# An AdaLN block with a routed and a shared feed-forward layer on one core: five experts instead of four are scattered to tables of their own, and the tables are loaded whole

## What is computed

```python
h = _layernorm(x, axis=-1) * (1 + cb) + sb          # after a causal running mean was added to x
logits = xf @ gate_weight.T                          # 8 experts
scores = softmax(logits).T
vals, idx = top_k(scores.reshape(-1), 2 * S)         # the 8192 best (expert, token) pairs of all
h = gelu(xf @ W1[e] + b1[e]); y = h @ W2[e] + b2[e]  # for each chosen pair, weighted by its score
shared = gelu(xf @ Ws1 + bs1) @ Ws2 + bs2            # for every token
x = x + gb * (routed + shared)
```

## Time and profile before

| | us |
|---|---|
| median of 3 executions | 339.92 |
| lowest, highest | 336.08, 343.24 |
| the profiled execution | 338.42 |
| its span | 336.5 |

### The profile page before, as it was taken

How to read it: one execution, slowest core, us unless ns; L and a number is a source line. 1 busy time by engine, 2 the same in 40 slices (tenths; PEclk the granted TensorE clock), 3 DMA queues, 4 the chain that set the end, 5 groups by cost and what they waited for, 6 DMA issues and landing times.

```text
span 336.5 us, 4143 instructions
## 1 busy us (share of the span) xinstructions
PE 259.8 (77%) x1033; PEld 138.9 (41%) x1033; DVE 177.7 (53%) x774; ACT 139.8 (42%) x238; POOL 196.5 (58%) x243
## 2 busy tenths in 40 slices
PE   4789777999999999999795996999999888700000
PEld 1657765443445454544352452544434334500000
DVE  2799865767656476567567567649351323100000
ACT  2768977454334434444333243344543443300000
POOL 7567862000026556567778770787878686868560
PEclk9999997999999999999999699799999999965555
DMA  7912991149962113123164272466884233333320
GB/s 190 341 37 78 314 317 76 31 99 228 133 254 59 36 41 105 44 51 114 52 211 137 78 265 83 162 230 181 301 294 39 25 33 31 32 39 32 31 24 8
DMA packets 25760, 40.72 MB, mean 121 GB/s; under 512 B 7544, under 2 KB 17599, under 8 KB 24704
## 3 DMA queue, kind: packets, MB, share of 16 engines
q1 hardware_dynamic: 17218, 31.09, 31.4%
q0 software_dynamic: 8384, 9.23, 15.2%
q10 hardware_dynamic: 126, 0.04, 0.0%
HBM read 22.62 MB, written 17.73 MB: 120 GB/s over the span
## 4 chain that ended last, share of the span: by engine, by line
PE 38%; POOL 24%; issue 11%; DMA 11%; DVE 9%; ACT 3%; POOLq 1%; SPq 0%; DVEq 0%; ACTq 0%
POOL out_dram L1166 14%; PE U L1311 8%; PE Y L1351 7%; POOL R L1141 6%; DMA INV<-sums_scratch 5%; PE U L1317 5%; PE Y L1355 5%; DMA out_dram<-YO,IDXB 4%; POOL sums_scratch L1154 3%; PE R1b L1199 2%; PE R L1199 2%; PE Y L1241 2%; DVE GJ L934 2%; PE R L1455 2%; DMA CST<-in_consts_dram 1%
## 5 line engine op out<-in xcount | busy, mean ns | idle before, releaser
L1141 POOL DMA_INDIRECT R<-rows_scratch,IDXB x68 | 69.0, 1014 | 70.8 <-DVE IDXB L950 52.2
L523 ACT ACTIVATE HF<-U,COL 128x512 f32<-128x512 f32 x96 | 65.8, 687 | 87.4 <-PE U L1317 56.0
L1166 POOL DMA_INDIRECT out_dram<-YO,IDXB x36 | 56.4, 1566 | 21.6 <-DMA out_dram<-YO,IDXB 12.1
L1317 PE MATMUL U<-XT,XW 128*128 128x512 f32 x128 | 66.6, 608 | 2.9 <-issue 2.9
L1355 PE MATMUL Y<-HF,XW 128*128 128x512 f32 x128 | 66.8, 614 | 0.0
L1154 POOL DMA_INDIRECT sums_scratch<-YO,IDXB x32 | 34.1, 1066 | 18.0 <-issue 9.1
L1311 PE MATMUL U<-H2F,WS 128*128 128x512 f32 x64 | 34.8, 627 | 0.0
L994 DVE SCALAR_TENSOR_TENSOR YO<-R1b,R,GBR 128x128 f32<-128x128 f32 x64 | 18.0, 344 | 30.6 <-DMA out_dram<-YO,IDXB 26.2
L1317 PEld LDWEIGHTS U<-XT,XW 128*128 128x128 f32 x128 | 23.1, 195 | 26.8 <-issue 23.6
L1351 PE MATMUL Y<-HF,WS 128*128 128x512 f32 x64 | 33.8, 610 | 0.0
L1355 PEld LDWEIGHTS Y<-HF,XW 128*128 128x128 f32 x128 | 23.2, 197 | 19.2 <-issue 19.2
(11 more groups left out here) (217 smaller groups left out, 369.1 us busy)
## 6 DMA issues: line engine op xcount, KB each, us to landing
sums_scratch<-R SPq DMA_DIRECT2D x8, 1024.0 KB, 6.4
INV<-sums_scratch SPq DMA_DIRECT2D x16, 512.0 KB, 4.9
XW<-in_wx_dram SPq DMA_DIRECT2D x10, 512.0 KB, 5.7
XW<-in_L_attn_x_dram SPq DMA_DIRECT2D x8, 256.0 KB, 6.9
rows_scratch<-HT SPq DMA_DIRECT2D x8, 256.0 KB, 4.0
out_dram<-X SPq DMA_DIRECT2D x4, 512.0 KB, 7.0
R<-rows_scratch,IDXB POOLq DMA_INDIRECT x68, 2.7
INV<-in_inv_dram SPq DMA_DIRECT2D x3, 256.0 KB, 6.7
```

The source lines that it names most:

```text
L523: eng.activation(HF[:, g % RING, :], UB[g % 2][:, :], ACT.Gelu_apprx_tanh, bias=B1[:, at:at + 1]).then_inc(M["a_gelu"], 1)
L1141: eng.indirect_dma_start(XG[:, v % XR, s, :], None, rows_dram, bass.IndirectOffsetOnAxis(ap=IDXB[:, v, s:s + 1], axis=0)).then_inc(M[f"ld_ ...
L1166: eng.indirect_dma_start(out, bass.IndirectOffsetOnAxis(ap=IDXB[:, v, s:s + 1], axis=0), YO[:, v % YR, s, :], None, compute_op=ALU.add).th ...
L1317: eng.matmul(bank[:, :], weights(v, 0, c, 0), XT[:, v % 2, :], start=True, stop=True).then_inc(M["pe_up"], 1)
```

## The change

A fifth expert gets a table (NTAB 5), so units 0 to 9 scatter plainly and units 10 to 16 accumulate. Two more clears of 1 MB are issued ahead. Each quarter of a table has a buffer of its own: two in INV, two in H2F, over shared blocks 0 to 3, whose last reader is waited for; so a whole table is loaded at once, a quarter waiting only for the add of the same quarter of the table before. The adds stand at the steps that ADD_AT names and the loads at LOAD_AT. The jobs are reordered: shared block 6 follows unit 9 and shared block 7 follows unit 10, so `close(6)` and `close(7)` come later, at steps 71 and 79. The last table's adds stand at steps 78 and 79. The lists come each five half steps. Six units are gathered ahead of the first scatter (AHEAD 6), then two or three DMAs for each scatter (5 for two), and behind the scatter of unit 9 all that are left, 22.

```diff
--- before.py
+++ after.py
@@ -36,12 +36,11 @@
 ROW = D + E + 1
 NPAD = BLK
 XR = 12
-NTAB = 4
+NTAB = 5
 YR = 4
-TBR = 2
 PAIR = 2 * BLK
 NP = NB // 2
-AHEAD = 9
+AHEAD = 6
 WR = 4
 LAG = 2
 
@@ -53,8 +52,8 @@
 H0 = max(BIT_AT) + 1
 
 ALONE = NMAIN - 4
-JOBS = ([(0, b) for b in range(NB - 2)] + [(1, 0), (1, 1), (0, NB - 2), (1, 2), (1, 3), (0, NB - 1)]
-        + [(1, v) for v in range(4, NU)])
+JOBS = ([(0, b) for b in range(NB - 2)] + [(1, v) for v in range(2 * NTAB)]
+        + [(0, NB - 2), (1, 2 * NTAB), (0, NB - 1)] + [(1, v) for v in range(2 * NTAB + 1, NU)])
 SJ = [JOBS.index((0, b)) for b in range(NB)]
 UJ = [JOBS.index((1, v)) for v in range(NU)]
 FIRST = NC * UJ[0]
@@ -66,18 +65,31 @@
 
 FAR = 32768.0
 K_MASK, K_TIE, K_CUM, K_DQ, K_IDX = 0, 1, 2, 5, 6
-MASK_AT = {K_IDX + 2 + 6 * (v - 1): v for v in range(1, NMAIN)}
+MASK_AT = {K_IDX + 2 + 5 * (v - 1): v for v in range(1, NMAIN)}
 EXTRA = 10
-K_OVER = K_IDX + 2 + 6 * (EXTRA - 1) + 3
+K_OVER = K_IDX + 2 + 5 * (EXTRA - 1) + 3
 OV_DONE = 10
 
 TR = 5
 CLOSE_AT = {21: 0, 23: 1, 25: 2, 27: 3, 28: 4, 29: 5, NC * SJ[6] + 7: 6, NC * SJ[7] + 7: 7}
 PART0 = 5
 
+
+ADD_AT = {}
+for e, at in enumerate((UJ[6], UJ[8], SJ[6], SJ[7])):
+    for q in range(NP):
+        ADD_AT[NC * (at + q // 3) + q % 3] = [(e, q)]
+ADD_AT[NC * UJ[11] + 2] = [(NTAB - 1, 0), (NTAB - 1, 1)]
+ADD_AT[NC * UJ[11] + 3] = [(NTAB - 1, 2), (NTAB - 1, 3)]
+
+LOAD_AT = {NC * UJ[5] + 3: 0, NC * UJ[7] + 3: 1, NC * UJ[9] + 3: 2, NC * UJ[10] + 3: 3, NC * UJ[11] + 1: 4}
+STORE_AT = NC * UJ[11] + 2
+
+ADDED = {6: 3 * NP, 7: 4 * NP}
+CLOSED = [6, 6, 6, 7, 8]
+
 XC0 = NB - 3
 NHT = 3
-PER_GAP = 2
 
 ROWS_AT = {3: NB - 3, 5: NB - 2, 7: NB - 1}
 
@@ -86,13 +98,13 @@
 
     if v >= 2 * NTAB - 1:
         return NT * NMAIN
-    return max(NT * AHEAD + PER_GAP * (v + 1), NT * (v + 4))
+    return NT * AHEAD + 5 * (v + 1) // 2
 
 
 
 SEMS = """ld_cst ld_uc ld_few ld_rows ld_x0 ld_x1 ld_x2 ld_x3 ld_x4 ld_x5 ld_x6 ld_x7 ld_wmod ld_ws ld_irow ld_inv1 ld_inv
 ld_wu0 ld_wu1 ld_wu2 ld_wu3 ld_xg0 ld_xg1 ld_xg2 ld_xg3 ld_xg4 ld_xg5 ld_xg6 ld_xg7 ld_xg8 ld_xg9
-ld_tb0 ld_tb1 ld_xg10 ld_xg11
+ld_tb0 ld_tb1 ld_tb2 ld_tb3 ld_xg10 ld_xg11
 st_z st_tz st_ht0 st_ht1 st_ht2 st_sc st_out st_sc0 st_sc1 st_sc2 st_sc3
 pe_inv pe_few pe_cols pe_mod pe_gbc pe_cbr pe_t1 pe_t3 pe_t4 pe_t6 pe_lg pe_up pe_dn pe_out pe_sum pe_tie pe_cum pe_dq
 pe_ov pe_idx pe_xt pe_yt pe_stc
@@ -166,7 +178,6 @@
         ZERO = sb("ZERO", [P, BLK])
 
         INV = sb("INV", [P, NT, BLK])
-        TB = INV[:, :, :].rearrange("p (k t) c -> p k (t c)", k=TBR)
         WS = sb("WS", [P, 2 * F])
         WMOD = sb("WMOD", [P, 6 * D])
         ROWS = sb("ROWS", [P, P])
@@ -193,6 +204,9 @@
         CLEAR = R1[:, 3 * PAIR:5 * PAIR]
         X2 = sb("X2", [P, NB, BLK])
         H2F = sb("H2F", [P, S])
+
+        TB = [INV[:, 2 * q:2 * q + 2, :].rearrange("p t c -> p (t c)") for q in range(2)] + [
+            H2F[:, q * PAIR:(q + 1) * PAIR] for q in range(2)]
         HT = sb("HT", [P, NHT, BLK])
         HF = sb("HF", [P, RING, BLK])
         TMP = sb("TMP", [P, TR, BLK])
@@ -360,12 +374,16 @@
                 if q == 0:
                     for v in (2 * e, 2 * e + 1):
                         eng.wait_ge(M[f"st_sc{v % YR}"], 64 * (v // YR + 1))
-                if NP * e + q >= TBR:
-                    eng.wait_ge(M["v_add"], NP * e + q - TBR + 1)
+                if e:
+                    eng.wait_ge(M["v_add"], NP * (e - 1) + q + 1)
+                elif q < 2:
+                    eng.wait_ge(M["v_ct"], NB)
                 else:
-                    eng.wait_ge(M["v_ct"], NB)
-                eng.dma_start(TB[:, q % TBR, :].rearrange("p (t c) -> p t c", c=D),
-                              by_partition(sums[e])[:, 2 * q * NT:2 * (q + 1) * NT, :]).then_inc(M[f"ld_tb{q % TBR}"], 16)
+                    eng.wait_ge(M["pe_up"], NC * SJ[3] + NC)
+                    eng.wait_ge(M["pe_t6"], NB)
+                    eng.wait_ge(M["pe_lg"], NB)
+                eng.dma_start(TB[q].rearrange("p (t c) -> p t c", c=D),
+                              by_partition(sums[e])[:, 2 * q * NT:2 * (q + 1) * NT, :]).then_inc(M[f"ld_tb{q}"], 16)
 
             def store_base(q):
                 eng.wait_ge(M["v_add"], NP * (NTAB - 1) + q + 1)
@@ -391,15 +409,12 @@
                     load_expert(v // 2 + WR - 1)
                 if c == 2 and v == NS - 4:
                     load_pair(NS)
-                if c == 3 and v >= 4 and v % 2 == 0 and v // 2 - 2 < NTAB:
-                    for b in range(TBR):
-                        load_sums(v // 2 - 2, b)
-                if c == 0 and v >= 5 and v % 2 and v // 2 - 2 < NTAB:
-                    for b in range(TBR, NP):
-                        load_sums(v // 2 - 2, b)
-                if c == 3 and v == 2 * NTAB + 3:
-                    for b in range(NP):
-                        store_base(b)
+                if s in LOAD_AT:
+                    for q in range(NP):
+                        load_sums(LOAD_AT[s], q)
+                if s == STORE_AT:
+                    for q in range(NP):
+                        store_base(q)
             eng.wait_ge(M["v_used"], 1)
             used = eng.value_load(USED[0:1, 0:1], min_val=NMAIN, max_val=NU)
             pair(NMAIN)
@@ -786,16 +801,19 @@
             def close(b):
                 eng.wait_ge(M["pe_out"], b + 1)
                 eng.wait_ge(M["v_x2"], b + 1)
+                if b in ADDED:
+                    eng.wait_ge(M["v_add"], ADDED[b])
                 eng.tensor_tensor(X2[:, b, :], RB[1][:, :], X2[:, b, :], ALU.add).then_inc(M["v_out"], 1)
 
             def add_sums(e, q):
-                eng.wait_ge(M[f"ld_tb{q % TBR}"], 16 * (NP // TBR * e + q // TBR + 1))
+                eng.wait_ge(M[f"ld_tb{q}"], 16 * (e + 1))
+                eng.wait_ge(M["v_out"], min(2 * q + 2, CLOSED[e]))
                 if e:
                     eng.wait_ge(M["v_add"], NP * (e - 1) + q + 1)
-                else:
-                    eng.wait_ge(M["v_out"], 2 * q + 2)
+                elif q == NP - 1:
+                    eng.wait_ge(M["v_x2"], NB)
                 at = X2[:, 2 * q:2 * q + 2, :].rearrange("p b s -> p (b s)")
-                eng.tensor_tensor(at, TB[:, q % TBR, :], at, ALU.add).then_inc(M["v_add"], 1)
+                eng.tensor_tensor(at, TB[q], at, ALU.add).then_inc(M["v_add"], 1)
 
             def ties(k):
                 TF = C_I.bitcast(F32)
@@ -1019,9 +1037,8 @@
                     close(CLOSE_AT[s])
                 half_step(2 * s + 1)
                 v, c = unit_step(s)
-                if v >= 5 and v % 2 and v // 2 - 2 < NTAB and c in (1, 2):
-                    for b in range((c - 1) * TBR, c * TBR):
-                        add_sums(v // 2 - 2, b)
+                for e, q in ADD_AT.get(s, ()):
+                    add_sums(e, q)
                 if v >= 0:
                     if c == 1 and v == NS - 2:
                         biases(NS)
```

## The result

The changed kernel takes 328.69 us (median; 328.11 to 329.4) against 340.16 of the kernel before in the same comparison: the ratio is 0.970, 95% interval 0.961 to 0.979. The forecast was 321 and faster, in a range of 312 to 333. So the direction and the range held, and the gain is 0.6 of what was forecast: 11.5 us, not 19.2. The profiled execution took 329.4, its span is 327.6.

The account below looks back on a forecast made before the run. GpSimd's full queue was taken as the bound, TensorE only its supplier. From 338.42 us, 17.2 came off for the shorter accumulating tail and 0.7 for its earlier start: 320.5, stated as 321, range 312 to 333.

Parts of the forecast that it names:

- The pair less at the end: Accumulating tail on GpSimd: units 8 and 9 leave it, 28 DMAs of 36 remain, saving 17.2 us of 86.0.
- T: Time when GpSimd starts to accumulate: forecast 249.8 us, 0.7 before the old 250.54.
- Start: GpSimd's first plain scatter: six units gathered ahead instead of nine, so it starts at 132 us instead of 154.2.
- This is the only slip of the queue, 2.1: GpSimd's queue before unit 8's scatter: YO ready at about 203.9 us, wanted at 201.8; no other late YO expected.
- Price of the adds: VectorE's 20 table adds lengthen GpSimd's queue before T by 0.42 us each, 8.4 in all.
- TensorE's waits: TensorE waits for gathered rows of units 9 and 11, some 6.5 us and 4 us, before steps 59 and 71.
- The base path: Last adds done at 242.8 us, store landing 7.0 later: 249.8, within half a microsecond of GpSimd's queue at 249.3.
- VectorE's loads: VectorE's waits for table loads, 18.8 us at ten of sixteen adds before, were costed at nothing.
- GpSimd idles again as before 210.83: Rival: one more GpSimd hole of 8.2 us before T, T at 258, time 329; inside the range, no separate chance.
- VectorE becomes the bound: Rival: VectorE late at all five tables, GpSimd holes of 41 us, T up to 284, time 355; chance 0.08.
- Nothing slips: Rival: adds cost nothing and TensorE doesn't stall, T 241.3, time 312; faster than the forecast band had 0.06.
- the worst price for each add: Rival: each add stops GpSimd 1.05 us, queue 12.6 us longer, T 261.9, time 333; chance 0.07.

Follow-up runs that it names:

- The experiment: Each of the 20 table adds cut to 8 of its 1024 columns, against the changed kernel, loads and waits kept: 322.61 us, 0.963 of the kernel before.

## Why the prediction was right or wrong

**The pair less at the end: right.** 86.0 - 17.2 = 68.8 was forecast, 69.2 measured, and 69.0 to 69.2 in five more profiles with 28 accumulating DMAs and whole adds (69.2 to 70.6 in the three with cut adds); 86.0 to 87.1 with 36.

**T: the step that failed.** Forecast 249.8, measured 258.36. By its terms:

- *Start*, 132 forecast, 134.07 measured: 2.1. The first gather was already 1.9 late (see the last section); six units took 34.1 from there, against the 34 that were worked out.
- *"This is the only slip of the queue, 2.1"*: wrong. The holes are 7.0 net, 4.9 more. I worked out YO's time for units 0, 6, 8 and 9 and gave the cover of unit 6, 6.8 us, to all. Unit 3's falls behind the overflow's arithmetic and a list, unit 5's behind the adds of the first table and a list, both on VectorE. That VectorE is full was said, but for steps 48 to 59 and as a sum over them; what counted was what stood ahead of one YO. The hole before unit 8 was the one forecast (2.1, measured 3.1). With its gap it is 3.40, more than the 3 us that the prediction had named as a sign that it is wrong. That the first two holes come from what stood ahead of each YO is read from VectorE's rows; no run moved the overflow's arithmetic.
- *Price of the adds*, 0.42 each, from the rows of before. Without the holes the stretch from the first scatter to T holds 10.5 more than its gathers and scatters, against 8.4. The experiment gives 0.47 for an add, so most of this term was right; 1.1 of it is not the adds'.

These three are 9.1, and from 249.3, the queue's T, they lead to 258.4.

**TensorE's waits: right in length.** 6.5 and 4.6 us at the rows of units 9 and 11 were forecast, 7.04 and 4.48 measured. In part that is luck: TensorE arrived for unit 9 at 193.4, not 186.7, and the rows were there at 200.5, not 193.2, so both sides of the difference came some 7 us late. The sum gave the first wait its share in one slip of 2.1 and no other. The version with three gathers each takes the second wait away and shortens the first, and is 2.4% faster than the changed kernel (0.9475 to 0.9703), though by the holes before units 3 and 5 too.

**The base path: right in kind.** Both paths to T were to meet, at 249.8. In the changed kernel the last store was issued at 252.1 and landed at the latest 4.6 later (not 7.0), 256.7, 1.7 ahead of T. The adds ahead of it were forecast done at 242.8 and were done 9 us later: 8.0 of that is the rows of unit 11, there at 230.5 instead of 222.5, since their gather stands in the same late queue. So the base path hangs on the queue, and was not a second, independent bound:

```profile
L390 SPq DMA_DIRECT2D out_dram<-X x4: 332/335/338, 244.0 to 252.1; - x4
...
DMA to landing us min/median/max: 2.6/4.5/4.6
```
With the adds cut this path is the later one, by 1.6, and with lists each six half steps by 0.5.

**VectorE's loads: right.** Asked for its waits, the line of the adds (L816, 20 of them) shows no idle time of VectorE that a load ended, where it was 18.8 us in the earlier trace rows.

**Rivals.** "GpSimd idles again as before 210.83", 329: its time came, but its mechanism only in part, since 4.9 of the 9.1 are holes, in three places instead of one. "VectorE becomes the bound" happened in small: 3.9 us of the holes net (units 3 and 5) are VectorE's, against 17.9 at which it would have decided. "Nothing slips" and the worst price for each add did not come.

## What to carry to other kernels

Lay an in-order queue out as a ledger, with waits for each producer apart, and then ask of each wait what it would turn into: here a faster producer of lists gave nothing, because the time came back as waits for the other producer. Work out the arrival for every item of the queue and not for three of them; the ones that share a step with rare work (an overflow, a table's adds) are those that are late. When a queue has mandatory work that can stand anywhere, put it where it covers late items: half a gather more behind each scatter added nothing to GpSimd's work and gave 2.4%, by a comparison across chips.

## What the runs showed that I had not expected

**TensorE's clock in front of the first gather.** Up to 58 us the changed kernel is 0.6 ahead, and from 64 us on it is 1.9 behind. The window from 53 to 60 us, changed and then before:

```profile
core 0: us, PE busy (x) PEld busy (x) DVE busy (x) ACT busy (x) POOL busy (x), PEclk, DMA share, GB/s
53.00:60.00 7.00, 6.10 (x16) 3.29 (x17) 4.16 (x20) 4.00 (x8) 1.63 (x7) 0.50 0.00 0
```
```profile
53.00:60.00 7.00, 6.02 (x23) 3.33 (x22) 4.44 (x21) 5.21 (x9) 1.63 (x7) 0.76 0.00 1
```
The granted clock (third number from the right) is 0.50 there instead of 0.76, the lower one of 1.2 and 2.4 GHz for the whole window; from 60 to 66 us it is 0.75 instead of 1.00. An up product takes 2.05 us there (at 57.72) instead of 1.10 (at 58.36 before). TensorE is busy for 6.10 and 6.02 of the 7 us, with the same work for it in both programs. Of nine profiles of the changed kernel and its variants six have 0.50 to 0.60 in that window and three 0.76; of five of the kernel before and its variants four have 0.76 and one 0.91. What makes the lower clock likelier with the changed program was not found, nor whether more profiles would keep the difference.

**Chips.** The kernel before took 338 on two chips and 365 to 368 on two others, and there a change that is worth 3% gave 1%, with an interval that holds 1. With six units ahead instead of nine the kernel before was 1.8% slower there; whether a full queue bridges pauses only as far as it has work ahead was not tested on a chip without them.
